# One pipeline over eight chunks for output projection, layer norm, shared expert and routing; expert weights split during the experts' stage; routing transfers moved

## The chip, the cores and the metric

The kernel runs on one core of one Trainium2 chip. The metric is device time in microseconds (us), the median of three runs. A profile is one execution recorded by the hardware profiler; its span runs from the first to the last instruction.

The engines are TensorE (PE; its weight loads are PEld), VectorE (DVE), ScalarE (ACT), GpSimd (POOL) and SyncE (SP), which here only issues transfers (its queue is SPq). TensorE has a granted clock of two levels, 1.2 and 2.4 GHz, written 0.50 and 1.00.

## What is computed

Two transformer layers on 4 x 1024 tokens of width 256, all in float32:

```python
x = x + attn0(layernorm(x))      # 16 heads of 16, causal softmax, then  o @ W_O.T
x = x + ffn0(layernorm(x))       # 32 experts, grouped top-8, latent width 128, plus a shared expert
x = x + attn1(layernorm(x))      # linear attention with decay, 16 heads of 128, RMS norm, gate
x = x + ffn1(layernorm(x))       # 48 kept experts of 128, top-8, capacity 96

# ffn0, what matters here
scores = sigmoid(x @ gate_w.T);  sb = scores + gate_bias
group_scores = top_k(sb grouped 4 x 8, 2).sum();  2 of 4 groups stay;  top 8 of the rest
w = scores at the top 8, divided by their sum, times 2.5
x_lat = x @ fc1_w.T
h = relu(x_lat @ w1[e].T)**2 * w[e]          # for each of 32 experts
routed = (sum over e of h @ w2[e].T) @ fc2_w.T
shared = relu(x @ shared_up_w.T)**2 @ shared_down_w.T
```

## The kernel before

Each stage is a `Phase`: it owns its tiles and semaphores, and at its end all engines meet at a barrier. Inside a phase each engine has its own instruction list, ordered by hand, and semaphores tie the lists together. The 4096 tokens are 32 tiles of 128 rows (`X[128, 32, 256]`, resident), or 8 chunks of 512. A float32 matrix product is made of three products of halves: the operand copied to `F32R` (the "high" part, on ACT) and the rest (the "low" part, a subtraction on DVE or POOL).

In the middle of the kernel stand these phases, one after the other:

- `trA` (`transpose_phase`, L230 to L262): the attention's output `AO` is transposed, all 8 chunks, into high and low halves.
- `proj` (`output_phase`, L789 to L811): the product with W_O for 32 tiles, each added to `X`.
- `lnB` (`transpose_phase`): mean and variance (L182, L185), square root on ACT (L245), normalised rows (L254), transposes (L230), halves (L262, L203).
- `shared` (`shared_phase`): per chunk the latent product and four inner products (L906), relu and square on ACT (L882, L887), then the second product (L923, full float32, recorded as two matmuls each), added to `X` (L962). After the last chunk come the gate's logits, 192 matmuls that stream 32 columns each (L940), and one sigmoid (L895).
- `route` (`group_routing_phase`): on DVE a chain of some forty operations over all 32 tiles at once (L1047 to L1090), each waiting for the one before; beside it the 4 MB of expert weights come in eight loads (L1020) and are split by ACT (L1104) and POOL (L1032). The square roots of the weights are transposed (L1096) and stored to `B_roots` (L1024).
- `experts` (`experts_phase`): for each of 8 chunks and 32 experts, three `up` matmuls (L1250 to L1252), weighing by roots and squaring (L1176, L1222, L1223, low part L1183 on DVE or, each fourth, L1210 on POOL), three `down` matmuls (L1259 to L1265). The roots come as 64 broadcast loads of 1 MB (`experts_sq`, L1150), four buffers ahead. The fc2 weight is loaded behind the first four of them (L1155), and PE waits for it before the loop. Twice a chunk `out` multiplies by fc2 (L1273).
- `lnC` and `lin`: the second attention, untouched in its loops. At its end DVE adds the 32 tiles of the result to `X` (L1666).
- `rank` (`ranking_phase`): an eight-chunk pipeline already. SP's list begins with the gate weight, the store of all of `X` to `out` (L1790) and the zero fills of `out`, `token_rows` and `odd_sums` (L1792 to L1797), and only then the stores of the normalised rows (L1803), which free the two `lines` buffers of ACT (L1980). DVE builds the one-hot tile `A` with twelve compares (L2081).
- `kept`: gather, products and scatter of the 48 experts, untouched.

## Time and profile before

| | us |
|---|---|
| median of three runs (3235.17 to 3238.91) | 3237.99 |
| the profiled execution | 3233.19 |
| its span | 3231.4 |
| attention of layer 0, start to 652 | 652 |
| trA, proj, lnB, shared, route: 652 to 952 | 300 |
| experts: 952 to 1358 | 406 |
| lnC, lin: 1358 to 2890 | 1532 |
| rank: 2890 to 3042 | 152 |
| kept: 3042 to the end | 189 |

Stage limits are read from the first and last instructions of each phase. Views list groups by line and engine, instructions in order of time, or busy time by stretch; "[x <-y]" at the end of a row is the idle time before it and what ended it. Busy times of pipelined matmuls overlap, so PE's pace is read from the distance of their starts.

### The profile page before, as it was taken

How to read it: one execution, taken by the hardware profiler on the slowest of the kernel's cores; microseconds unless marked ns; L12 is line 12 of the kernel's file. 1: busy time of each engine (PE TensorE's matmuls, PEld its weight loads, DVE VectorE, ACT ScalarE, POOL GpSimd, SP SyncE). 2: the span in 40 equal slices, each digit the busy share in tenths (PEclk: the TensorE clock that was granted, in tenths of full speed). 3: DMA queues.
4: the chain of work that ended last, by engine and by line, in shares of the span. 5: the costliest groups of instructions: out<-in, count | busy, mean ns of one | idle time of the engine just before them, and what ended most of it. 6: DMA issues, size and time to landing. Idle time of an engine off the chain costs nothing. (4 is left out here: it accounts for less than half of the span.)

```text
span 3231.4 us, 51793 instructions
## 1 busy us (share of the span) xinstructions
PE 2842.1 (88%) x17676; PEld 2278.6 (71%) x17676; DVE 1793.6 (56%) x3257; ACT 1451.9 (45%) x2661; POOL 773.7 (24%) x797
## 2 busy tenths in 40 slices
PE   5599999968918999879999999999999999967484
PEld 4544444457916878668888888888888888856463
DVE  5288888552166878755555555555555545554421
ACT  5247777744126877643333333333333333324110
POOL 2411222200021222112222222222222222213575
PEclk9889999978758999979999999999999999975665
DMA  4875555000037999500000000000000000023376
GB/s 149 231 100 71 73 74 81 3 19 0 1 90 157 178 184 174 119 11 10 10 10 2 8 10 10 10 10 10 10 10 9 1 10 10 8 68 98 74 173 125
DMA packets 183382, 193.61 MB, mean 60 GB/s; under 512 B 18080, under 2 KB 135360, under 8 KB 182720
## 3 DMA queue, kind: packets, MB, share of 16 engines
q1 hardware_dynamic: 174736, 177.10, 26.2%
q0 software_dynamic: 8544, 15.22, 2.8%
q8 instruction: 55, 0.90, 0.1%
q14 instruction: 47, 0.39, 0.1%
HBM read 149.89 MB, written 46.58 MB: 61 GB/s over the span
## 5 line engine op out<-in xcount | busy, mean ns | idle before, releaser
L744 DVE TENSOR_REDUCE score_pm<-score_SM 128x1 f32<-128x512 f32 (+3 forms) x608 | 364.5, 656 | 123.9 <-PE score_SM L613 73.7
L1423 POOL TENSOR_TENSOR lin_o2sum<-lin_o2sum,lin_o 128x512 f32<-128x512 f32 x128 | 165.7, 1295 | 1046.9 <-ACT lin_o L1459 1046.9
L704 ACT ACTIVATE score_PR<-score_SE 128x512 f32<-128x512 f32 (+1 forms) x640 | 309.9, 557 | 105.6 <-PE score_SE L638 102.1
L1638 DVE SCALAR_TENSOR_TENSOR lin_go<-lin_gT,lin_O 128x512 f32<-128x512 f32 x128 | 88.1, 688 | 477.8 <-ACT lin_o L1459 477.8
L1494 PE MATMUL lin_PJ<-C_XH,lin_WH 128*128 128x512 f32 x1032 | 341.6, 412 | 13.1 <-DVE lin_WL L1598 13.1
L1494 PE MATMUL lin_PJ<-C_XH,lin_WL 128*128 128x512 f32 x1032 | 320.5, 392 | 0.0
L1494 PE MATMUL lin_PJ<-C_XL,lin_WH 128*128 128x512 f32 x1032 | 320.4, 392 | 0.0
L610 PE MATMUL score_SM<-score_KR,score_QR 96*128 96x512 bf16 (+3 forms) x768 | 230.1, 341 | 28.3 <-DMA score_V<-v_rows 25.5
L1655 DVE TENSOR_TENSOR lin_acc<-lin_OUT,lin_acc 128x512 f32<-128x512 f32 x256 | 177.1, 692 | 139.9 <-PE lin_OUT L1529 138.7
L1442 ACT ACTIVATE lin_qT<-lin_PJ 128x512 f32<-128x512 f32 x129 | 77.1, 598 | 378.5 <-PE lin_PJ L1494 378.5
L1494 PEld LDWEIGHTS lin_PJ<-C_XL,lin_WH 128*128 128x128 f32 x1032 | 194.0, 188 | 43.2
L1494 PEld LDWEIGHTS lin_PJ<-C_XH,lin_WL 128*128 128x128 f32 x1032 | 194.0, 188 | 42.7
L1650 DVE TENSOR_TENSOR lin_gol<-lin_go,lin_goh 128x512 fp32r<-128x512 f32 x128 | 200.6, 1567 | 24.4 <-ACT lin_goh L1464 14.7
L638 PE MATMUL score_SE<-score_QR,score_KR 99*128 99x512 bf16 (+3 forms) x768 | 210.5, 330 | 2.0 <-ACT score_PR L704 1.5
L1222 ACT ACTIVATE experts_h<-experts_z 128x512 f32<-128x512 f32 x256 | 161.1, 629 | 109.5 <-DVE experts_z L1176 89.3
L1494 PEld LDWEIGHTS lin_PJ<-C_XH,lin_WH 128*128 128x128 f32 x1032 | 175.6, 190 | 34.7 <-DVE lin_WL L1598 13.5
L1176 DVE SCALAR_TENSOR_TENSOR experts_z<-experts_HP,experts_sq 128x512 f32<-128x512 f32 x256 | 172.2, 686 | 49.7 <-PE experts_HP L1252 26.7
L1560 PE MATMUL lin_O<-lin_sd,lin_v 128*128 128x128 f32 x1024 | 190.9, 276 | 6.3 <-issue 6.3
L1418 POOL TENSOR_TENSOR lin_qd<-lin_qT,lin_dec 128x512 f32<-128x512 f32 x128 | 166.0, 1297 | 84.3 <-DVE lin_dec L1620 73.9
L1562 PE MATMUL lin_O<-lin_qd,lin_kv 128*128 128x128 f32 x896 | 173.2, 275 | 0.0
L1560 PEld LDWEIGHTS lin_O<-lin_sd,lin_v 128*128 128x128 f32 x1024 | 159.7, 191 | 18.9 <-issue 9.7
L1210 POOL TENSOR_TENSOR experts_hl<-experts_h,experts_hh 128x512 fp32r<-128x512 f32 x64 | 83.0, 1296 | 344.5 <-ACT experts_hh L1223 336.8
(342 smaller groups left out, 6444.8 us busy)
## 6 DMA issues: line engine op xcount, KB each, us to landing
experts_sq<-B_roots SPq DMA_DIRECT2D x64, 1024.0 KB, 16.8
score_QR<-q_parts SPq DMA_DIRECT2D x96, 128.0 KB, 7.0
score_KR<-k_parts SPq DMA_DIRECT2D x96, 128.0 KB, 7.7
kept_GU<-L_ffn_gate_up_proj SPq DMA_DIRECT2D x48, 192.0 KB, 2.9
v_rows<-qkv_vt SPq DMA_DIRECT2D x32, 256.0 KB, 2.6
score_V<-v_rows SPq DMA_DIRECT2D x16, 512.0 KB, 10.8
C_w<-L_attn_w_qkv SPq DMA_DIRECT2D x51, 128.0 KB, 2.2
q_parts<-qkv_parts SPq DMA_DIRECT2D x16, 384.0 KB, 2.7
```

What stands on the lines that cost most here:

```text
L610: ins = nc.tensor.matmul(SM[:, count % RING, at:at + nk], QR[0:ROWS_QK, u, h0 + j, t * P:(t + 1) * P], KR[0:ROWS_QK, u, h0 + j, k0:k0 + nk ...
L638: ins = nc.tensor.matmul(SE[:, e % RING, at:at + nq], KR[0:ROWS_ALL, u, h, kt * P:(kt + 1) * P], QR[0:ROWS_ALL, u, h, q:q + nq], start=Tru ...
L704: nc.scalar.activation(PR[:, st % BUFS, h, 0:width], SE[:, e % RING, 0:width], ACT.Exp, scale=SCALE)\
L744: nc.vector.tensor_reduce(pm[:, n % 2, h0:h0 + nh, t, k0 // CHUNK], SM[:, count % RING, 0:nh * nk].rearrange("p (h k) -> p h k", h=nh), AX ...
L1176: nc.vector.scalar_tensor_tensor(z[:, e % 2], HP[:, e % BUFS], 0.0, sq[:, (e // QE) % BUFS, e % QE], ALU.max, ALU.mult).then_inc(dve_z, 1)
L1418: nc.gpsimd.tensor_tensor(qd[:], qT[:, u], dec[:, 0:1, :].to_broadcast([P, B4, BLK]), ALU.mult).then_inc(pool_qd, 1)
L1423: nc.gpsimd.tensor_tensor(o2sum[:, c], o2sum[:, c], o2[:], ALU.add).then_inc(pool_sum, 1)
L1494: ins = nc.tensor.matmul(PJ[:, bank], a[:, w, k, :], x[:, k, :, c, :], start=(n == 0), stop=(n == 3 * KD - 1))
L1560: ins = nc.tensor.matmul(O[:, b, :], v[:, b, :], sd[:, b, :], start=True, stop=(c == 0))
L1562: ins = nc.tensor.matmul(O[:, b, :], kv[:, b, :], qd[:, b, :], start=False, stop=True)
L1650: nc.vector.tensor_tensor(gol[:], go[:], goh[:].bitcast(F32), ALU.subtract).then_inc(dve_gol, 1)
L1655: nc.vector.tensor_tensor(dst, OUT[:, half], dst, ALU.add).then_inc(dve_acc[half], 1)
```

## The change

1. `output_phase`, the `lnB` transposes, `shared_phase` and `group_routing_phase` become one `front_phase`. In step i of ten, PE handles chunk i (transpose of AO, projection), chunk i-1 (transpose of the normalised rows, gate logits) and chunk i-2 (latent, inner and second products). The logits are made transposed, as 32 rows by 512 columns, so six 512-column matmuls a chunk replace 24 of 32 columns; the sigmoids are transposed back. Routing runs on DVE in four batches of 8 tiles, its pieces laid between the other work of the steps.
2. The expert weights: the first eight experts are loaded during `front`; the other loads, and all splits, are in `experts`. POOL does most of them in the first chunk. fc2 is loaded in `front` too.
3. The zero fills go to `front`; the ranking gate's loads go to `lnC`; the store of `X` to `out` is done by chunk, each behind the store of that chunk's rows.
4. The last addition of `lin` moves into the ranking stage, two chunks at a time ahead of their statistics. The twelve compares of `A` become one `tensor_tensor`.

```diff
+def front_phase(nc, a, AO, X, LH, LL, first_w, roots, ident, out, odd, rows):
+        @block.sync: loads wo, wu (2), wg, down, bias, then first_w (w1, w2 of experts 0 to 7, fc2), the four zero fills,
+            for c in range(CHUNKS):
+                sp.wait_ge(act_ro, c + 1)
+                sp.dma_start(roots[:, c * CHUNK:(c + 1) * CHUNK], rootT[:, c % 2])...
+        @block.tensor
+            for i in range(STEPS):                       # CHUNKS + 2
+                at_a, at_n, at_f = now(i, 0), now(i, 1), now(i, 2)
+                rooting = i - 5 if i >= 5 and i % 2 else None
+                attended(at_a)                           # 8 transposes of AO
+                latent(at_f); inner(at_f, 0); inner(at_f, 1)
+                normalised(at_n)                         # 8 transposes, waits lines_ready
+                inner(at_f, 2); inner(at_f, 3)
+                root_columns(rooting)                    # waits roots_ready
+                projection(at_a)
+                gates(at_n)
+                root_columns(rooting + 1)
+                second(at_f)
+                score_rows(at_n, i)
+            root_columns(CHUNKS - 2, CHUNKS)
+            root_columns(CHUNKS - 1, CHUNKS)
+        @block.vector
+            for i in range(CHUNKS + 1):
+                starts = (i - 3) // 2 if i >= 3 and i % 2 else None
+                ends = (i - 4) // 2 if i >= 4 and i % 2 == 0 else None
+                attended_low(at_a); latent_low(at_f)
+                group_sums(starts); refined_roots(starts - 1)
+                top_experts()                            # ends
+                low(at_n)
+                add_projection(at_a); variances(at_a)
+                add_second(at_f, 0); group_ranks(); add_second(at_f, 1)
+                scales(at_a); group_masks()
+                add_second(at_f, 2); add_second(at_f, 3); shares(ends)
+            last, b = CHUNKS - 1, CHUNKS // 2 - 1
+            latent_low(last); group_sums(b); refined_roots(b - 1); add_second(last, 0); group_ranks()
+            group_masks(); add_second(last, 1); top_experts(); add_second(last, 2); shares(b)
+            add_second(last, 3); refined_roots(b)
...
 def experts_phase
-            for q in range(BUFS):
+            load(0, 0)
+            load_weights(1, 0)
+            load_weights(1, 1)
+            for q in range(1, BUFS):
                 load(0, q)
-            sp.dma_start(fc2[:], a["L0_ffn_fc2_w"]).then_inc(w_in, 16)
+            (load_weights(2, w) behind dve_wl, load_weights(3, w) behind pool_wl)
...
+            for w, e in LOWS[0:4]:                       # POOL, chunk 0: 12 lows, 8 highs, between its eight `low`
+                weight_low(w, e)
+            low(0, 3)
+            weight_high(0, 16)
...
+            for q in range(2):                           # ACT, before its loop
+                for w in range(2):
+                    if q == 1:
+                        act.wait_ge(raw_in[q * 2 + w], 16)
+                    nc.scalar.activation(HIGH[w][:, q * WG:(q + 1) * WG, :], wraw[:, q, w], ACT.Copy)...
...
 def linear_attention_phase
-            for t in range(TILES):
-                nc.vector.scalar_tensor_tensor(X[:, t, :], acc[:, t, :], rs[:, t:t + 1], X[:, t, :],
-                                               ALU.mult, ALU.add)
 def ranking_phase, SP
-            sp.dma_start(o2n[0], o2n[1]).then_inc(o_loaded, 16)
-            sp.dma_start(raw[0], raw[1]).then_inc(g_loaded, 16)
-            sp.dma_start(out[0:T, :].rearrange("(t p) n -> p t n", p=P), X[:]).then_inc(stored, 16)
-            (the four zero fills)
             for i in range(STEPS): ... store of lines, chunk g
+                    sp.wait_ge(x_ready, (g + 1) * TPC)
+                    sp.dma_start(out[g * CHUNK:(g + 1) * CHUNK, :]..., X[:, tiles_of(g), :])
 def ranking_phase, DVE
             def variances(run):
                 for t in tiles:
+                    nc.vector.scalar_tensor_tensor(X[:, t, :], acc[:, t, :], rs[:, t:t + 1], X[:, t, :],
+                                                   ALU.mult, ALU.add).then_inc(x_ready, 1)
+                for t in tiles:
                     nc.vector.bn_stats(stats[:, t, :], X[:, t, :]).then_inc(stats_ready, 1)
             variances(0)
+            scales(0)                                    # was behind the seven casts and `perm`
-                    for v in range(HI):
-                        ins = ts(A[:, g % 3, :, v, :], ..., float(v), None, ALU.is_equal)
+                    tt(A[:, g % 3], places.to_broadcast([P, TPC * EG, HI, 8]),
+                       step_no[:].to_broadcast([P, TPC * EG, HI, 8]), ALU.is_equal).then_inc(dve_a, 1)
```

## Rows read from the trace of the kernel before

**Rows 1.** The page: busy time of each engine over the whole span.
```profile
PE 2842.1 (88%) x17676; PEld 2278.6 (71%) x17676; DVE 1793.6 (56%) x3257; ACT 1451.9 (45%) x2661; POOL 773.7 (24%) x797
```

**Rows 2.** Busy time by stretch; lnB, shared, route, experts.
```profile
core 0: us, PE busy (x) PEld busy (x) DVE busy (x) ACT busy (x) POOL busy (x), PEclk, DMA share, GB/s
702.00:738.00 36.00, 15.71 (x64) 12.54 (x64) 23.31 (x81) 25.29 (x45) 0.00 (x0) 0.51 0.11 32
738.00:890.00 152.00, 148.19 (x688) 131.69 (x688) 20.76 (x42) 46.74 (x76) 0.00 (x0) 0.87 0.00 0
890.00:952.00 62.00, 6.48 (x32) 4.45 (x32) 46.28 (x130) 14.85 (x14) 20.49 (x8) 0.53 0.27 77
...
981.00:1357.00 376.00, 372.06 (x1607) 301.06 (x1608) 293.01 (x458) 287.52 (x512) 81.69 (x63) 0.99 0.86 167
```

**Rows 3.** PE in order of time: transposes, projection, inner products, second product.
```profile
663.61 1.09 PE L230 MATMUL trA_tr<-ident,trA_rows 128*128 128x128 f32 x8 [0.76 <-DVE A_XL L203]
681.30 0.46 PE L800 MATMUL proj_Y<-proj_WH,A_XH 128*128 128x256 f32 x2
...
682.80 0.46 PE L800 MATMUL proj_Y<-proj_WH,A_XH 128*128 128x256 f32 x2
...
835.13 0.62 PE L906 MATMUL shared_HP<-B_XH,shared_WH 128*128 128x512 f32 x2
835.59 0.62 PE L906 MATMUL shared_HP<-B_XL,shared_WH 128*128 128x512 f32 x2
...
837.86 13.97 PE L923 MATMUL shared_OP<-B_w_down,shared_su 128*128 128x256 f32 x64
```

**Rows 4.** Busy time by stretch, inside the shared stage: before and in the logits.
```profile
837.00:851.00 14.00, 14.00 (x66) 12.29 (x65) 2.98 (x7) 3.43 (x5) 0.00 (x0) 1.00 0.00 1
...
856.00:889.00 33.00, 32.64 (x154) 32.53 (x153) 0.00 (x0) 0.33 (x1) 0.00 (x0) 0.50 0.00 0
```

**Rows 5.** Groups by line, 700 to 1150 us: costs that the steps repeat.
```profile
L203 DVE TENSOR_TENSOR B_XL<-lnB_tr,B_XH 128x1024 fp32r<-128x1024 f32 x8 | 9.8, 1223 | 10.1 <-ACT B_XH L262 10.1
...
L962 DVE TENSOR_TENSOR X<-shared_OP,X 128x256 f32 (+1 forms) x32 | 13.6, 425 | 72.6 <-PE shared_OP L923 72.6
...
L1087 DVE RECIPROCAL route_inv<-route_root 128x1024 f32<-128x1024 f32 x1 | 6.6, 6552 | 1.1 <-ACT route_root L1106 1.1
...
L895 ACT ACT_TABLE_LOAD x1 | 1.3, 1283 | 0.0
```

**Rows 6.** DVE and POOL in order of time in the routing stage.
```profile
896.51 2.60 DVE L1052 TENSOR_TENSOR route_hi<-route_hi 128x256 f32<-128x256 f32 x1
...
901.63 0.42 DVE L1054 TENSOR_TENSOR route_u<-route_lo 128x256 f32<-128x256 f32 x1
...
896.49 4.83 POOL L1032 TENSOR_TENSOR B_W1L<-route_raw,B_W1H 128x1024 fp32r<-128x1024 f32 x2 [257.79 <-ACT B_W1H L1104]
```

**Rows 7.** Experts: PE's first wait, and two stretches, one of them in routing.
```profile
982.49 0.79 PE L1250 MATMUL experts_HP<-B_LH,B_W1H 128*128 x1 [23.83 <-DMA experts_fc<-L_ffn_fc_w]
...
1165.00:1210.00 45.00, 44.58 (x190) 34.77 (x189) 34.18 (x55) 34.11 (x62) 9.78 (x8) 1.00 1.01 184
...
900.00:922.00 22.00, 0.00 (x0) 0.00 (x0) 21.31 (x93) 5.49 (x6) 14.51 (x6) 0.50 0.49 143
```

**Rows 8.** End of lin and head of rank, in order of time: DVE, SP, ACT, PE.
```profile
2876.66 12.75 DVE L1666 SCALAR_TENSOR_TENSOR X<-lin_acc,lin_rs,X 128x256 f32<-128x256 f32 x32
...
2902.34 15.94 SPq L1797 DMA_DIRECT2D odd_sums<-rank_zero  x1
...
2927.73 2.08 ACT L1980 ACTIVATE rank_lines<-X,rank_shift,rank_rstd 128x256 f32<-128x256 f32 x4 [21.28 <-DMA token_rows<-rank_lines]
...
2903.35 1.94 PE L1905 MATMUL rank_tr<-ident,rank_lines 128*128 128x128 f32 x8 [4.90 <-ACT rank_lines L1980]
...
2932.11 1.94 PE L1905 MATMUL rank_tr<-ident,rank_lines 128*128 128x128 f32 x8 [16.24 <-DVE rank_XL L2073]
...
2959.90 2.80 DVE L2081 TENSOR_SCALAR rank_A<-rank_hi 128x192 bf16<-128x192 bf16 x12
```

877 lines of the change are left out of this document (556 added, 321 removed).

## Prediction, made before the changed kernel was built or timed

> **What bounds the kernel now.** The page first: PE is busy 88% of the span [rows 1], so the time to be won is where PE is idle, at half clock, or on work that costs more than it must. The view by stretch shows where [rows 2]. From 652 to 952 us lie five stages in a row, and each has another limit: in trA and lnB PE, ACT and DVE hand a chunk round (in lnB PE is busy 16 of 36 us, at a clock of 0.51); in the shared stage PE is the bound (148 of 152 us); in routing PE does 6.5 of 62 us while DVE works off its chain. Within the shared stage the clock tells of waste: it is 1.00 while products of 256 and 512 columns run, and 0.50 through the logits, though PE is busy 32.6 of 33 us there [rows 4]; those 192 matmuls of 32 columns last from 851.5 to 889, about 37 us. The experts' stage is bound by PE (clock 0.99, busy 372 of 376 us), with the transfers just behind: a DMA share of 1.01 at 184 GB/s in the middle [rows 7]. Ahead of it stands a wait of 23.8 us for the small fc2 weight, which is queued behind 4 MB of roots [rows 7]. In rank, ACT waits 21.3 us for a `lines` buffer, because SP is stuck for 15.9 us issuing a zero fill [rows 8].
>
> **Part 1, the front pipeline.** What PE must do for one chunk at full clock, from starts [rows 3]: eight transposes 1.1 us, twice (2.2); the projection, two tiles in 682.80 - 681.30 = 1.50, so four tiles 3.0; latent, four inner and the gates, six groups of six 512-column matmuls 0.227 apart (835.59 - 835.13 = 0.46 for two), 6 x 1.36 = 8.2; the second product, 64 records from 837.86 in 13.97 us, so 32 in 6.8 (its last 0.2 overlap); scores and roots, eight small transposes, at most 1.1. Sum 21.3 us; I take 21.2 for a full step.
>
> Do the others fit under it? DVE per step: the two low halves 2 x 1.22 and the latent one 0.69, projection and second additions 8 x 0.425 = 3.4 [rows 5], variances and scales about 2.4 (estimated: half of lnB's 3.5 us for eight tiles, and some waits): 8.9. The routing: DVE is busy 46.3 us in the routing stage [rows 2]. Of this about 10 us is not work: L1052 takes 2.60 us where L1054, the same shape, takes 0.42, and it starts with a POOL subtraction of 2.4 us (two take 4.83) [rows 6]; five operations in the view are longer by 2.0 to 2.2 us in this way. 36 / 4 = 9 us for a batch of 8 tiles, plus about forty times 0.1 us, since small operations don't shrink with their size: 13 to 14 us per two steps. They aren't even: odd steps hold the sums, ranks, masks and refined roots (a reciprocal of 6.55 / 4 = 1.6 us [rows 5] among them), some 9.5, even steps 4.8. DVE is then at 18.4 of 21 in odd steps, 13.7 in even ones. ACT: halves 2.0, latent 0.6, four relu and square 4.9, sigmoid 0.6, rows 2.1, roots and copies 1.3, sqrt 0.2 and, as the work alternates between sigmoid and sqrt, two table loads of 1.28 [rows 5]: 14.3. So PE stays the bound.
>
> Where the lists touch: in odd steps from 5 on PE waits with `root_columns` for DVE's refined roots. Behind them on DVE stand the shares of the last step (to 2.7 us into the step), the two low halves (4.6), the sums (8.0) and the roots (11.1), while PE is there at 8.7: 2.4 us lost, in steps 5 and 7. Queued behind PE's wait are projection, gates and second product, all of them. The normalised rows are ready at the step's end and wanted 5 us into the next, so that handover is hidden; without that cover the 2.4 would grow by what it is late.
>
> The stretch, step by step. Steps 0 and 1 have no products of a third chunk to hide anything: loads and splits of W_O (about 5.5 us), projection at half clock 5.1, statistics and rows 5.6, transposes, halves, projection, gates, scores 11: 27.5 us, step 2 starts at 680. Steps 2 to 7: 6 x 21.2 + 2 x 2.4 - 1.6 (no roots yet in the first three) = 130, to 810. Step 8 has no new chunk: 16.6, to 827. Step 9 and the tail go by DVE: second product begun at 11, ranks, masks, top 8 and shares of the last batch between the additions to 22, refined roots 25.5, two transposes and copies 28, store and barrier 31.3: 858. The first root load of the experts' stage, now at 952.8, comes at 858: **95 us less**. Bounds: 108 less if steps cost 19.5 us (starts overlap better) and the tail 27; 60 less if each of seven steps costs 5 us more.
>
> **Part 2, the experts.** Removed: the wait for fc2 (23.8 us), during which the root buffers stay full or arrive unused. Added: 6 weight loads of 0.5 MB in the first chunk, and splits on ACT, DVE and POOL ahead of it or in it. Price of a load: the routing stage moved 143 GB/s at a share of 0.49 [rows 7], so 290 GB/s when busy, 1.8 us each, 11 us in all. Roots: 1.05 MB at 184 GB/s = 5.7 us each; the first four took 6.7 (982.49 less 952.8 and 2 us for the first to come, by 4.1 MB). The first chunk needs eight of them and the weights: 2 + 8 x 6.1 + 11 = 62 us, where PE's work is 44: it is bound by transfers. The other 56 root loads follow at 5.7 us (PE's own pace for four experts is 4 x 6 x 0.227 + 0.2 = 5.65, so it can't be faster by much): 319. Then the last four experts and the tail, 14: 395 us against 405 now. **10 less**; bounds +5 (roots at 160 GB/s in the first chunk and every later stall kept) to 20 less (PE as the only bound after 16 us). ACT's loop starts behind the second pair of weight loads, about 14 us in; this is under the roots' arrival. POOL's 12 lows, 8 highs and 8 own lows at 1.3 us are 36 of 62 us. DVE's low halves will at times wait as L1052 did, 24 x up to 1.3 us: DVE 19 + 24 x 1.9 = 65 us at the very worst, 3 us over the transfers. I take 0.
>
> The Trainium skill ("SBUF — State Buffer", Who interferes with whom) speaks against this edit: a DVE operation with two inputs in SBUF and a GpSimd operation that reads SBUF shut each other out for a whole instruction. By that rule, the trace agrees (2.60 against 0.42 us), and in the first chunk the sum would be 3 us longer.
>
> **Part 3, rank.** Now: roots of the RMS norm ready at 2876.6, 12.75 us of additions [rows 8], barrier, first transposes at 2903.35, third group at 2932.11 after a 16.2 us wait. After: barrier to 2878, memset 0.9, eight additions 3.2, statistics 3.5, scales: first rows at 2886. PE's list first needs the permuted gate, behind casts and `variances(1)` with another 3.2: transposes at 2896, second 2900, third 2909. From there as now, 109 us, plus some 3 us for the additions of later runs: end at 3021 instead of 3041. **20 less.** The cover: the out stores, now one 0.5 MB store per chunk, 2 to 4 us in steps of 11. If they block as now, it is 4 less instead of 20. `A` costs 2.80 us in twelve compares [rows 8]; one operation of 2304 elements costs from 1.3 to 2.5 us, plus up to 3.1 when POOL's product is in flight (twelve short ones meet it too, up to 4.7 us in the last chunks); I take 0, bounds -1.5 to +1 per chunk, DVE having 4 us spare per step. Zero fills in the front: 4.3 MB beside no other transfer, hidden. Gate loads in lnC, hidden.
>
> **Sum.** 95 + 10 + 20 = 125 us. The profiled execution has span 3231.4 and time 3233.2; so span 3106, time 3108. The median stands 4.8 above that execution: **3113 us**.
>
> **Rivals.** *Handovers rule the pipeline* (each of seven steps 4 to 7 us longer, since nine waits of three hand-ordered lists are met in one order only): for it, the odd steps, where DVE has 2.6 us spare by my count; against it, the 5 us slack of the rows. 3113 + 28 to 49: about 3150. *The ranking stall moves instead of going*: 3113 + 16 = 3129. *The experts' transfers don't fit* (stall kept, or POOL late with the third weight group): 3113 + 15 = 3128. *Everything overlaps better* (13 in the front, 10 in the experts): 3090. *Slower than before*: the pipeline runs at half clock. Step 2 to the end of PE's work is 130 + 17 + 14 = 161 us at full clock; each of them at half costs as much again: 3113 + 161 = 3274. It takes a clock of 0.50 in 78% of it (125 of 161 us) to lose the whole gain. For it: lnB at 0.51 and the logits at 0.50 with PE busy [rows 2, 4]; against: the dense stretch at 1.00 [rows 4], which is made of the same matmuls, and the transposes and small groups are 1 to 2 us long between them. The Trainium skill ("TensorE: Matmul & The Clock Gate", HAM oscillation) says that a PE that pauses between bursts falls back to half clock again and again; the trace agrees in lnB, and it would make 3274 if each step paused long enough.
>
> **Chances.** Forecast 0.64 (own range 3095 to 3128), handovers 0.16, rank stall 0.06, experts 0.07, better 0.05, half clock 0.02. Range for 8 in 10: 3085 to 3150. A measurement can tell about 0.2% (6 us) from no change. Faster 0.97, the same 0.01, slower 0.02; the front alone would have to lose 95 us for the middle case.
>
> **What would show it.** Front: first root load at 858, steps 21.2 us apart by their gates, clock 1.00 from step 2 on, PE waiting only for refined roots in steps 5, 7 and 9. Experts: PE never waits for fc2 but for roots in the first chunk, which lasts 62 us; 395 us in all. Rank: no wait of ACT for `token_rows`, 145 us from the roots of the norm (2876.6 now) to the last index. It is wrong if steps exceed 25 us, if the clock is 0.50 inside them, or if later chunks of the experts lack roots by more than 15 us in all.

## The result and the profile after

The changed kernel takes 3124.61 us (median of 4 runs, 3122.50 to 3126.47), the kernel before 3238.15 us on the same chip (4 runs, 3235.17 to 3238.91): a ratio of 0.9651, 95% interval 0.9634 to 0.9668, or 113.5 us less. The forecast was 3113 us, range 3085 to 3150. The profiled execution took 3125.01 us with a span of 3123.2 us, against 3233.19 and 3231.4 before.

A stage is measured here from one event to the next: start, first root load of the experts, first load of the next layer norm, roots of the RMS norm ready, first load of the kept experts, end.

| stretch | before, us | after, us | difference | forecast |
|---|---|---|---|---|
| up to the first root load (the front) | 952.8 | 856.9 | -95.9 | -95 |
| experts | 406.8 | 416.6 | +9.8 | -10 |
| layer norm and linear attention | 1516.8 | 1518.0 | +1.2 | 0 |
| ranking (the additions are within it in both) | 166.2 | 142.6 | -23.6 | -20 |
| kept experts | 188.9 | 189.2 | +0.3 | 0 |
| sum | 3231.5 | 3123.3 | -108.2 | -125 |

Two of the three terms came within 4 us, the third has the wrong sign. These are single profiles: in the seven profiles whose front is the same code, the first root load comes at 856.6 to 859.7 us. These are the rows of the change. First the whole span, which answers to [rows 1]:

```profile
PE 2817.1 (90%) x17564; PEld 2237.4 (72%) x17564; DVE 1800.2 (58%) x3284; ACT 1463.9 (47%) x2689; POOL 792.0 (25%) x812
```

TensorE was busy 25 us less, and the span is 108 us shorter: three quarters of the gain is time in which TensorE had been idle. By stretch, the front (it answers to [rows 2]; start, length, busy time of PE, PEld, DVE, ACT, POOL, granted clock, DMA share, GB/s): its head, steps 2 to 7, step 8, step 9 with the tail.

```profile
652.00:680.00 28.00, 16.19 (x86) 14.36 (x87) 11.43 (x32) 11.21 (x15) 3.60 (x3) 0.67 0.85 251
680.00:808.00 128.00, 124.38 (x686) 103.73 (x684) 80.58 (x273) 83.50 (x132) 0.00 (x0) 1.00 0.02 4
808.00:825.00 17.00, 17.00 (x83) 13.26 (x81) 6.04 (x32) 8.58 (x13) 0.00 (x0) 1.00 0.00 0
825.00:857.00 32.00, 18.07 (x81) 12.92 (x79) 19.96 (x74) 9.92 (x17) 0.00 (x0) 0.86 0.04 9
```

The pace of the steps stands in TensorE's order of time, at the transposes that open each step, and, in odd ones, at those of the refined roots:

```profile
700.90 1.09 PE L936 MATMUL front_TR<-ident,AO 128*128 128x128 f32 x8
721.35 1.09 PE L936 MATMUL front_TR<-ident,AO 128*128 128x128 f32 x8
741.81 1.09 PE L936 MATMUL front_TR<-ident,AO 128*128 128x128 f32 x8
752.20 0.61 PE L1031 MATMUL front_RT<-ident,front_root 128*32 128x128 f32 x4 [1.42 <-DVE front_root L1277]
764.74 1.09 PE L936 MATMUL front_TR<-ident,AO 128*128 128x128 f32 x8
...
850.59 1.03 PE L1031 MATMUL front_RT<-ident,front_root 128*32 128x128 f32 x4 [6.59 <-DVE front_root L1277]
```

These are the openings of steps 3 to 6. Steps 3, 4 and 6 take 20.45 us, step 2 takes 21.4, steps 5 and 7 take 22.9. The last root transposes at 850.6 wait 6.6 us for VectorE; that is the tail.

In the experts' stage, the first chunk in order of time on POOL, PE and SP's queue, and then 45 us of the later chunks by stretch:

```profile
878.37 1.30 POOL L1451 TENSOR_TENSOR experts_hl<-experts_h,experts_hh 128x512 fp32r<-128x512 f32 x1 [2.48 <-ACT experts_hh L1513]
892.36 1.52 POOL L1461 TENSOR_SCALAR B_W1H<-B_wraw 128x512 fp32r<-128x512 f32 x1 [12.68 <-DMA B_wraw<-L_ffn_w]
...
896.65 1.26 POOL L1451 TENSOR_TENSOR experts_hl<-experts_h,experts_hh 128x512 fp32r<-128x512 f32 x1
...
897.97 0.79 PE L1564 MATMUL experts_Y<-experts_hl,B_W2H 128*128 128x512 f32 x1 [10.69 <-POOL experts_hl L1451]
...
858.62 11.59 SPq L1376 DMA_DIRECT2D experts_sq<-B_roots  x3
870.25 22.13 SPq L1380 DMA_DIRECT2D B_wraw<-L_ffn_w  x4
```

```profile
1065.00:1110.00 45.00, 44.44 (x191) 35.24 (x191) 36.70 (x58) 35.70 (x65) 9.21 (x8) 1.00 1.01 169
```

The 23.8 us of [rows 7] are gone. In their place TensorE waits 10.7 us for a low half of GpSimd (expert 7's), which stands in GpSimd's list behind the first copy of the third weight group; that copy waits 12.7 us for its transfer, and SyncE needs 22 us to issue four transfers. In the later chunks the DMA share is 1.01 at 169 GB/s; VectorE waited 25.0 us for roots from 927 to 1260 us, in 21 waits.

In ranking (it answers to [rows 8]): DVE, SP and PE in order of time, then the group of the comparison for `A`.

```profile
2793.79 3.20 DVE L2306 SCALAR_TENSOR_TENSOR X<-C_acc,C_rs,X 128x256 f32<-128x256 f32 x8
...
2803.30 0.37 SPq L2086 DMA_DIRECT2D token_rows<-rank_lines  x1
2803.73 0.50 SPq L2089 DMA_DIRECT2D out<-X  x1
...
2810.35 1.94 PE L2189 MATMUL rank_tr<-ident,rank_lines 128*128 128x128 f32 x8 [5.62 <-DVE rank_GL L2346]
...
2831.36 1.91 PE L2189 MATMUL rank_tr<-ident,rank_lines 128*128 128x128 f32 x8
2843.76 1.94 PE L2189 MATMUL rank_tr<-ident,rank_lines 128*128 128x128 f32 x8 [3.72 <-DVE rank_XL L2361]
```

```profile
L2369 DVE TENSOR_TENSOR rank_A<-rank_hi,rank_step_no 128x2304 bf16<-128x2304 bf16 x8 | 14.7, 1835 | 6.8 <-POOL rank_lo L2165 6.8
```

The same group in the kernel before, twelve a chunk:

```profile
L2081 DVE TENSOR_SCALAR rank_A<-rank_hi 128x192 bf16<-128x192 bf16 x96 | 30.4, 389 | 6.8 <-POOL rank_lo L1879 6.8
```

SyncE isn't held up any more, the first transposes come 19.0 us after the roots of the norm (2791.4) instead of 27.0, and the single comparison for `A` takes 1.84 us on average, where twelve took 3.8 (30.4 us in eight chunks; the 2.80 us of [rows 8] are one chunk of them, and they range from 1.5 to 5.6).

### The profile page after: what moved, and what is told of

Read it like the earlier page. It is cut to its first block and busy times, and to the rows that moved or that the text cites. A ratio compares the mean times of both kernels' runs of the same rounds, so it can differ in the third digit from the quotient of the medians.

```text
span 3123.2 us, 51426 instructions
## 1 busy us (share of the span) xinstructions
PE 2817.1 (90%) x17564; PEld 2237.4 (72%) x17564; DVE 1800.2 (58%) x3284; ACT 1463.9 (47%) x2689; POOL 792.0 (25%) x812
## 5 line engine op out<-in xcount | busy, mean ns | idle before, releaser
L1950 DVE TENSOR_TENSOR C_acc<-lin_OUT,C_acc 128x512 f32<-128x512 f32 x256 | 177.1, 692 | 141.9 <-PE lin_OUT L1824 139.6
L1737 ACT ACTIVATE lin_qT<-lin_PJ 128x512 f32<-128x512 f32 x129 | 76.9, 596 | 376.1 <-PE lin_PJ L1789 376.1
L1424 DVE TENSOR_TENSOR experts_hl<-experts_h,experts_hh 128x512 fp32r<-128x512 f32 x192 | 138.3, 720 | 49.7 <-ACT experts_hh L1513 40.7
## 6 DMA issues: line engine op xcount, KB each, us to landing
experts_sq<-B_roots SPq DMA_DIRECT2D x64, 1024.0 KB, 17.7
```

The lines of the kernel that those rows point to most:

```text
L1950: nc.vector.tensor_tensor(dst, OUT[:, half], dst, ALU.add).then_inc(dve_acc[half], 1)
```

## The experiments

The runs of one group share a chip with runs of the kernel before, whose median lay between 3233 and 3237 us in them; kernels of different groups are therefore compared by their ratio to it. Within the experts' stage, time is told by the copies of each chunk's sum (`experts_y`) on ScalarE: "first chunk" is from the first root load to the copy of chunk 0, "seven chunks" from there to the copy of chunk 7.

| kernel | median, us | ratio to before, 95% | first chunk | seven chunks | experts' stage |
|---|---|---|---|---|---|
| before | 3238.15 | 1 | 76.9 | 324.0 | 406.8 |
| changed | 3124.61 | 0.9651 (0.9634 to 0.9668) | 80.2 | 330.8 | 416.6 |
| pool_order | 3124.47 | 0.9649 (0.9633 to 0.9665) | 77.0 | 328.1 | 410.6 |
| sp_order | 3123.35 | 0.9647 (0.9631 to 0.9663) | 74.5 | 330.7 | 410.7 |
| two_groups | 3114.11 | 0.9617 (0.9601 to 0.9633) | 68.2 | 331.7 | 405.1 |
| half_roots | 3112.11 | 0.9612 (0.9596 to 0.9628) | 79.9 | 315.7 | 401.2 |
| distinct_rows | 3094.90 | 0.9574 (0.9558 to 0.9590) | 63.8 | 315.7 | 385.1 |
| chunk_major | 3095.33 | 0.9567 (0.9551 to 0.9583) | 62.7 | 315.7 | 383.9 |
| four_copies | 3107.39 | 0.9609 (0.9593 to 0.9625) | 73.8 | 315.7 | 395.0 |
| adds_back | 3123.42 | 0.9663 (0.9647 to 0.9679) | 79.8 | 325.0 | 410.3 |
| rank_back | 3143.60 | 0.9720 (0.9704 to 0.9736) | 80.2 | 328.5 | 414.3 |
| columns_late | 3123.37 | 0.9657 (0.9641 to 0.9674) | 79.5 | 327.2 | 412.2 |
| before_fc2_first | 3223.55 | 0.9972 (0.9962 to 0.9982) | 63.7 | 329.8 | 399.3 |
| before_chunk_major | 3210.97 | 0.9925 (0.9908 to 0.9941) | 61.0 | 317.5 | 384.2 |

The last three columns are from one profile each; in before_fc2_first they start at the load of fc2, 0.5 us ahead of the first root load. Three kernels leave something out of the result: two_groups half of the expert weights, half_roots half of the roots, distinct_rows all of the roots. Four kernels have the changed kernel's experts' stage word for word (changed, adds_back, rank_back, columns_late): it took 416.6, 410.3, 414.3 and 412.2 us. So the +9.8 us of the first table is +6.5 us on average (413.3 less 406.8), with a scatter of 3 us either way, nearly all of it in the seven later chunks; the first chunk repeats to 0.7 us. The kernel before has one profile only, and that execution lay 5 us under its median, so the loss itself is uncertain by some us: with the medians (113.5 us less) and all other stages as in the first table it would be 4.5 us.

### Why does the first chunk take 80 us?

pool_order puts two of GpSimd's own low halves first, and moves three later ones (15, 19 and 23) up with them.

```diff
             low(0, 3)
+            low(0, 7)
+            low(0, 11)
             weight_high(0, 16)
             weight_low(0, 16)
             weight_high(0, 20)
-            low(0, 7)
...
```

> The changed kernel with two of GpSimd's own low halves, of experts 7 and 11, put ahead of the first weight group it has to wait for. In the changed kernel the experts' stage lasts 416.6 us (first root load to the next layer's first load), of which the first chunk takes 80.2 us up to the copy of its sum. Theory A (the order alone: TensorE stands still for 10.7 us only because expert 7's low half is queued behind a weight copy that waits for its transfer): first chunk 70 us, whole kernel about 10 us faster than the changed one. Theory B (GpSimd has 33 us of work left from the landing of the third weight group at 892.4 us, so only an earlier landing helps): TensorE's wait moves to the later weight groups, first chunk 77 us, 3 us faster at most. Theory C (the first chunk is bound by transfers as a whole): 80 us, no change.

First chunk 77.0 us, theory B. The wait did not go, it moved. TensorE's rows, and one of VectorE's:

```profile
898.09 0.49 PE L1547 MATMUL experts_HP<-B_LH,B_W1H 128*128 x1 [1.57 <-POOL B_W1L L1470]
...
916.60 0.79 PE L1547 MATMUL experts_HP<-B_LH,B_W1H 128*128 x1 [3.62 <-POOL B_W1L L1470]
...
905.33 1.29 DVE L1417 SCALAR_TENSOR_TENSOR experts_z<-experts_HP,experts_sq 128x512 f32<-128x512 f32 x2 [5.62 <-DMA experts_sq<-B_roots]
```

TensorE now waits for low halves of later weights, and VectorE 5.6 us for the fifth root load, which SyncE could issue only behind the weight groups. Over the whole kernel nothing of it is left that can be measured (0.9649 against 0.9651).

sp_order leaves GpSimd's list alone and interleaves the loads.

```diff
             load(0, 0)
             load_weights(1, 0)
             load_weights(1, 1)
-            for q in range(1, BUFS):
-                load(0, q)
+            load(0, 1)
+            load_weights(2, 0)
+            load(0, 2)
+            load_weights(2, 1)
+            load(0, 3)
+            (load_weights(2, w) still behind dve_wl, load_weights(3, w) behind pool_wl)
...
+            (first round of the root loop written out, load_weights(3, w) behind its loads 0 and 1)
```

> The changed kernel with GpSimd's list as it was, but SyncE issues the third weight group between the first root loads instead of behind all four, and the fourth group between root loads five to seven. Theory A (order of GpSimd's list alone): the copy still waits for its landing, which is some 12 us earlier, so it gains too, about 10 us; it cannot be told from B here, but is by pool_order. Theory B (landing of the third group, then 33 us of GpSimd work): the third group lands at about 878 to 880 instead of 892, first chunk 68 us instead of 80.2, whole kernel 12 us faster. Theory C (first chunk bound by the bytes it moves, whatever their order): 80 us, no change.

First chunk 74.5 us, half of what theory B promised, and not theory C's 80:

```profile
883.72 1.95 POOL L1466 TENSOR_SCALAR B_W1H<-B_wraw 128x512 fp32r<-128x512 f32 x1 [1.17 <-DMA B_wraw<-L_ffn_w]
...
906.36 1.49 POOL L1466 TENSOR_SCALAR B_W1H<-B_wraw 128x512 fp32r<-128x512 f32 x1 [6.95 <-DMA B_wraw<-L_ffn_w]
...
909.13 0.79 PE L1569 MATMUL experts_Y<-experts_hl,B_W2H 128*128 128x512 f32 x1 [6.11 <-POOL experts_hl L1456]
```

The third group came early enough (a wait of 1.2 us), and now the fourth was late: GpSimd waits 7.0 us for it and TensorE 6.1 us for the low half behind it. In both orders some load is late. So the order of the queue is worth 6 us of this chunk and the order of GpSimd's list 3; the rest looks like a stretch limited by its transfers, which the later runs bear out. Both edits together were not run.

two_groups leaves half of the experts' weights out.

```diff
-            (load_weights(2, w), load_weights(3, w))
-            (weight_high(w, e), weight_low(w, e) for e of 16 to 31)
-                nc.tensor.matmul(HP[:, s], W1H[:, e, :], LH[:, cols], start=True, stop=False)
+                nc.tensor.matmul(HP[:, s], W1H[:, e % 16, :], LH[:, cols], start=True, stop=False)
...
```

> The changed kernel without the third and fourth weight groups: their four loads and GpSimd's twelve splits (eight high copies and eight low halves less the four of the second group) are left out, experts 16 to 31 are computed with the weights of 0 to 15, and the rest is as it was, so its output is not the reference's. It prices the split of the weights inside the experts' stage. Theories A and B: the first chunk falls from 80.2 to 60 to 64 us (16 us to the first product, then TensorE's own pace), 16 to 20 us faster. Theory C (bytes): 2 MB fewer at about 290 GB/s, 7 us faster. The later chunks stay at 330.8 us in all if their pace has nothing to do with the first chunk.

(GpSimd's instructions left out are sixteen, eight high copies and eight low halves, not twelve.) First chunk 68.2 us, 12.0 less: between the theories (16 to 20 by A and B, 7 by C). So loading and splitting half of the weights costs 12 us here; the two were not told apart. The seven later chunks stay at 331.7 us, as expected.

### What sets the pace of the later chunks?

half_roots takes half of the bytes away from the fifth root load on. (It was meant to begin with the second chunk; but `first` holds only for the four loads ahead of SyncE's loop, so the second half of the first chunk has half loads too.)

```diff
-                src = roots[q * QE:(q + 1) * QE, bass.ds(g * CHUNK, CHUNK)]
+                first = isinstance(g, int) and g == 0
+                n = QE if first else QE // 2
+                src = roots[q * QE:q * QE + n, bass.ds(g * CHUNK, CHUNK)]
...
```

> The changed kernel with only half of the bytes of each root load from the second chunk on: two of the four experts' roots are loaded, the other two are left from the first chunk, so its output is not the reference's. Copy of chunk 0 to copy of chunk 7 takes 330.8 us in the changed kernel (7 chunks of 47.3 on average, DMA share about 1.00 at 170 to 177 GB/s). If transfers set the later chunks' pace: they fall to TensorE's own 45 us, 313 to 316 us in all, 15 to 18 us faster. If the hand-over between TensorE, VectorE and ScalarE sets it: 328 to 331 us, no change. The first chunk stays at 80 us.

Seven chunks take 315.7 us instead of 330.8, and each of the five inner ones 45.34 or 45.35 us, where in the changed kernel they varied from 46.4 to 49.1. The transfers set the pace; TensorE's own is 45.35 us. The first chunk stays at 79.9 us though four of its eight root loads are halved: what delays it lies ahead of the fifth load.

distinct_rows brings as many bytes in as many pieces, from other addresses.

```diff
-                src = roots[q * QE:(q + 1) * QE, bass.ds(g * CHUNK, CHUNK)]
-                sp.dma_start(sq[:, q % BUFS], src.rearrange("(o e) n -> o e n", o=1).to_broadcast([P, QE, CHUNK]))\
+                src = distinct[q % BATCH].rearrange("(e p w) d -> p e w d", e=QE, w=2)
+                sp.dma_start(sq[:, q % BUFS].rearrange("p e (w d) -> p e w d", w=2), src)\
```

> The changed kernel in which each root load brings the same number of bytes in the same pieces (128 partitions, four pieces of 2 KB each), but every partition reads its own 2 KB of the kernel's input instead of all 128 reading the same 2 KB of roots; the mixture is weighed with wrong numbers, so its output is not the reference's. The later chunks take 330.8 us for seven in the changed kernel, 315.7 where half of the bytes were left out. Theory R (the repeated source is what holds the transfers at 170 to 184 GB/s): the loads get faster, seven chunks 316 to 319 us, whole kernel 12 to 15 us faster than the changed one. Theory B (the bytes into the partitions hold it, wherever they come from): 328 to 333 us, no change.

Theory R, and more of it than expected: 315.7 us for the seven chunks and 63.8 for the first, which none of the theories had put down to the source. So the bytes into the partitions, and the number of pieces, are not the limit; where they are read from is. Whether that is because all partitions read the same rows or because of how the rows lie in memory isn't shown by this run, which changes both and the tensor besides. An edit that keeps the result right, and all partitions reading the same rows, is chunk_major:

```diff
-        roots = nc.dram_tensor("B_roots", (EXPERTS, T), F32, kind="Internal").ap()
+        roots = nc.dram_tensor("B_roots", (CHUNKS * EXPERTS, CHUNK), F32, kind="Internal").ap()
...
-                sp.dma_start(roots[:, c * CHUNK:(c + 1) * CHUNK], rootT[:, c % 2]).then_inc(stored[c % 2], 16)
+                sp.dma_start(roots[c * E:(c + 1) * E, :], rootT[:, c % 2]).then_inc(stored[c % 2], 16)
...
-                src = roots[q * QE:(q + 1) * QE, bass.ds(g * CHUNK, CHUNK)]
+                src = roots[bass.ds(g * E + q * QE, QE), :]
```

> The changed kernel with the roots laid out in memory chunk by chunk, so that the four experts' roots of one load lie side by side: a partition reads one piece of 8 KB instead of four of 2 KB, still the same for all 128. Distinct sources took seven later chunks from 330.8 to 315.8 us. Theory P (16 DMA engines reading the same 2 KB at the same time hold each other up; over 8 KB they spread out): seven chunks 316 to 325 us, whole kernel 8 to 25 us faster than the changed one. Theory Q (what counts is that one place in memory serves all partitions, however long the piece): 326 to 333 us, no change.

Theory P, with all that could be had: ratio 0.9567 against 0.9651 for the changed kernel, 27 us of 3238 (a little more than the 25 that the theory allowed). One row each of the changed kernel, of distinct_rows and of chunk_major from the view of the DMA issues (count, size, median us from issue to landing); then 45 us by stretch, of distinct_rows and of chunk_major, and in chunk_major PE's wait for GpSimd in the first chunk (us in total, times, longest):

```profile
experts_sq<-B_roots SPq DMA_DIRECT2D x64, 1024.0 KB, 17.7
```

```profile
experts_sq<-L_attn_x SPq DMA_DIRECT2D x64, 1024.0 KB, 5.2
```

```profile
experts_sq<-B_roots SPq DMA_DIRECT2D x64, 1024.0 KB, 4.7
```

```profile
1065.00:1110.00 45.00, 45.00 (x200) 37.28 (x199) 37.10 (x58) 36.75 (x65) 10.35 (x8) 1.00 0.54 183
```

```profile
1065.00:1110.00 45.00, 45.00 (x201) 37.27 (x199) 37.44 (x58) 36.82 (x65) 10.01 (x9) 1.00 0.50 180
```

```profile
PE experts_Y L1564 <- POOL experts_hl L1451: 1.9, 3, 0.7
```

The same megabyte lands in 4.7 us instead of 17.7, and the DMA share of that stretch is 0.50 instead of 1.01 for a like rate. The 17.7 us contain the wait behind earlier loads that were still under way; the first root load of the stage, with none ahead of it, landed after 10.4 us in the changed kernel and 4.7 in chunk_major. PE waits 1.9 us in all for GpSimd in the first chunk instead of 11.4, and the chunk takes 62.7 us instead of 80.2, with GpSimd's list and SyncE's order unchanged. So the slow root loads, behind which the weights had to wait, made the first chunk long; the two orders only decided how much of that reached TensorE.

four_copies spreads the readers instead.

```diff
...
+                for k in range(COPIES):
+                    part = slice(k * P // COPIES, (k + 1) * P // COPIES)
+                    src = roots[k, q * QE:(q + 1) * QE, bass.ds(g * CHUNK, CHUNK)]
+                    src = src.rearrange("(o e) n -> o e n", o=1).to_broadcast([P // COPIES, QE, CHUNK])
+                    sp.dma_start(sq[part, q % BUFS], src).then_inc(sq_in[q % BUFS], 16)
```

> The changed kernel with four copies of the roots in memory, and each root load split in four transfers of 32 partitions, each from a copy of its own. 1.5 MB more is stored in the front, in eight steps. If repetition of an address over the whole load is what costs (128 readers of one row, now 32): seven chunks 316 to 325 us, whole kernel 8 to 25 us faster. If what costs is that the 16 engines read the same rows at the same moment (they take the four transfers one after the other, so they still do): 326 to 333 us, no change or, with the stores in the tail of the front, 1 to 2 us slower.

```profile
1065.00:1110.00 45.00, 45.00 (x200) 37.28 (x199) 37.12 (x58) 36.56 (x65) 10.34 (x8) 1.00 0.77 187
```

The seven chunks are at TensorE's pace here too, by a DMA share of 0.77, so four copies with a quarter of the readers each help as well; the first chunk (73.8 us) gains less than half as much as with the new layout. Why the old source is slow isn't settled by this. Readers per row, readers at one moment, the length of a piece (2 or 8 KB) and the 16 KB from one expert's row to the next were not told apart: chunk_major changes the last two together, four_copies the first together with the size of a transfer (256 KB).

### Was the wait for fc2 lost time?

before_fc2_first is the kernel before with one load moved.

```diff
+            sp.dma_start(fc2[:], a["L0_ffn_fc2_w"]).then_inc(w_in, 16)
             for q in range(BUFS):
                 load(0, q)
-            sp.dma_start(fc2[:], a["L0_ffn_fc2_w"]).then_inc(w_in, 16)
```

> The kernel before with one edit: the small fc2 weight is loaded ahead of the four root loads instead of behind them, so TensorE's 23.8 us wait goes. The stage lasted 406.8 us. Theory S1 (transfers set the pace of the whole stage, the wait for fc2 lay beside 4 MB of roots that had to come anyway): 402 to 407 us, whole kernel 0 to 5 us faster. Theory S2 (the wait is TensorE's own lost time, as the prediction has it): TensorE starts 13 us earlier and the stage ends 13 us earlier, at 394 us. It tells besides why seven later chunks took 324.0 us before and 330.8 after: 324 again if it is the place of the data in memory, 329 or more if it is that the transfers have no head start any more.

399.3 us, 7.5 less by one profile each; the medians of ten and thirteen executions on one chip differ by 9.7 us (3233.21 and 3223.55; 5.8 to 12.3 by the interval of the ratio), which is more than S1 allows. So it is between S1 and S2: the wait was worth 7.5 to 10 us. TensorE's first chunk ends 13.2 us earlier (63.7 against 76.9 us), and the seven others then take 329.8 instead of 324.0, so part of the thirteen is given back; how much isn't fixed by one profile, since the seven chunks of the changed kernel's code scatter from 325.0 to 330.8. VectorE's waits from 950 to 1030 us show where:

```profile
DVE experts_z L1176 <- DMA experts_sq<-B_roots: 15.1, 6, 8.7
```

Against 8.0 us in one wait from 952 to 983, and none from 983 to 1040, in the kernel before. While TensorE stood, the four buffers had filled; without that head start it runs into the transfers.

before_chunk_major gives the kernel before the new layout of the roots (the load as in chunk_major, the store in pieces of two chunks).

> The kernel before with the roots laid out in memory chunk by chunk, as in chunk_major, and nothing else changed; fc2 is still loaded behind four root loads, and all weights are still split in the routing stage. Its experts' stage lasted 406.8 us, that of the changed kernel 416.6 and with the new layout 383.9. It tells what the change's edits to the experts' stage are worth once the root loads are out of the way. Theory K (the old layout hid what the change wins there; freed of it the wait for fc2 shrinks to a few us by itself, since four loads take some 5 us each to land): the stage takes 380 to 386 us, as long as in the changed kernel or a little less, so those edits win nothing in this stage in either layout, and the whole kernel is 21 to 27 us faster than before. Theory L (the fc2 wait stays TensorE's own loss of 13 us or more, and with the loads out of the way the change wins the 10 us that the prediction gave it): the stage takes 392 to 396 us.

384.2 us, theory K, and the whole kernel 24 us faster. The wait for fc2 has shrunk by itself:

```profile
965.90 0.79 PE L1251 MATMUL experts_HP<-B_LH,B_W1H 128*128 x1 [8.09 <-DMA experts_fc<-L_ffn_fc_w]
```

With the new layout the experts' stage takes 384.2 us before the change and 383.9 after. So what the change does there wins no time in this stage in either layout. What it does bring is that three quarters of the loads and all splits of the weights no longer stand in the front, and with the new layout that costs nothing.

### Ranking and the odd steps

adds_back returns the additions to the end of the linear attention:

```diff
+            for t in range(TILES):
+                nc.vector.scalar_tensor_tensor(X[:, t, :], acc[:, t, :], rs[:, t:t + 1], X[:, t, :],
+                                               ALU.mult, ALU.add)
...
             def variances(run):
-                (the additions of this run, and the wait for them)
```

> The changed kernel with the 32 additions of the linear attention's result put back to the end of its stage, out of the ranking; everything else of the ranking as changed. From the roots of the norm to the end of the ranking the changed kernel takes 142.6 us, the kernel before 165.9 (23.3 less). Theory D (the additions and the transfers each have their share): 12.75 us of additions come back ahead of all, two times 3.2 go from the first tiles' path, so 150 to 155 us, 9 to 13 us slower than the changed kernel. Theory T (the transfers account for all of it, the additions only moved): 143 to 146 us.

145.3 us (2785.6 to 2930.9), 2.7 more than changed: theory T. Three of its rows show why it is so little:

```profile
2785.98 12.76 DVE L1961 SCALAR_TENSOR_TENSOR X<-C_acc,C_rs,X 128x256 f32<-128x256 f32 x32
...
2811.01 1.94 PE L2192 MATMUL rank_tr<-ident,rank_lines 128*128 128x128 f32 x8 [2.45 <-DVE rank_GL L2345]
...
2840.74 1.94 PE L2192 MATMUL rank_tr<-ident,rank_lines 128*128 128x128 f32 x8 [0.17 <-DVE rank_XL L2360]
```

The first transposes come 25.4 us after the roots of the norm, against 19.0: 6.4 us are lost at the head. But from the fourth transposes to the fifth it takes 8.9 us (2831.88 to 2840.74), where the changed kernel takes 12.4 (2831.36 to 2843.76), since a run of eight additions lies between them there: 3.5 us come back.

rank_back returns the transfers as well:

```diff
+            sp.dma_start(out[0:T, :].rearrange("(t p) n -> p t n", p=P), X[:]).then_inc(stored, 16)
+            (the four zero fills, taken out of the front)
...
-                    sp.dma_start(out[g * CHUNK:(g + 1) * CHUNK, :].rearrange("(t p) n -> p t n", p=P),
-                                 X[:, tiles_of(g), :]).then_inc(stored, 16)
```

> The changed kernel with the additions put back as in adds_back and also the zero fills and the one 4 MB store of the result put back to the head of the ranking's transfers. Both theories: the wait of ScalarE for its rows is back, about 166 us from the roots of the norm to the end of the ranking, 20 to 24 us slower than the changed kernel. Theory D: the difference to adds_back is 11 to 16 us, theory T: 20 us or more. If the single comparison for the one-hot table matters too, it ends a few us below 166, since that edit stays: 158 to 164.

```profile
2816.61 16.31 SPq L2085 DMA_DIRECT2D odd_sums<-rank_zero  x1
```

```profile
ACT rank_lines L2265 <- DMA token_rows<-rank_lines: 21.6, 1, 21.6
```

161.7 us, 16.4 more than adds_back and 19.1 more than changed, a little under the 20 to 24 of both theories; the 16.4 is just past theory D (11 to 16) and well short of theory T (20 or more). So adds_back came out as T had it and this one as D had it: the additions cost little, the transfers 16 us, and the rest is neither. SyncE's block of 16.3 us and ScalarE's wait of 21.6 us are those of [rows 8]. It ends 4.5 us short of the kernel before (166.2). Of this 1.6 us lie ahead of the first transposes (25.4 after the roots instead of 27.0). The gate's load, also moved, isn't what they waited for, since the permuted gate comes later here than in the kernel before (21.5 us after the roots, 20.7 before); the rows of ScalarE come earlier, 19.4 us after the roots instead of 23.0, since `scales(0)` and the rows now stand ahead of the casts and of the gate's copy. This order was not run by itself. Another 3.1 us lie behind the third transposes (107.2 to the end instead of 110.4), where the comparison for `A` is the only edit left.

columns_late moves the transposes of the refined roots.

```diff
-                if rooting is not None:
-                    root_columns(rooting, min(i - 1, CHUNKS))
                 if at_a is not None:
                     projection(at_a)
                 if at_n is not None:
                     gates(at_n)
+                (root_columns(rooting, min(i - 1, CHUNKS)) in steps 5 and 7)
...
                 (the second group inside second(), ahead of its second tile)
```

> The changed kernel with the transposes of the refined roots put later in TensorE's list in the odd steps: the first group behind the gates instead of ahead of the projection, the second behind the first tile of the second product. In the changed kernel an odd step of 5 and 7 takes 22.9 us and an even one 20.45; of the 2.5 us between them 1.4 us is TensorE's wait for VectorE's roots and about 1.1 us the transposes themselves. Theory W (only the wait is lost time, and nothing else is late behind it): steps 5 and 7 take 21.5 us each, the front 2.8 us less. Theory V (VectorE's list is what sets the odd steps): the wait comes back at another line, projection or second product, and the steps stay at 22.9 us.

```profile
741.09 1.09 PE L936 MATMUL front_TR<-ident,AO 128*128 128x128 f32 x8
752.95 0.51 PE L964 MATMUL front_YO<-front_WOH,front_AH 128*128 128x256 f32 x2 [1.50 <-DVE X L1200]
...
764.11 1.09 PE L936 MATMUL front_TR<-ident,AO 128*128 128x128 f32 x8
```

Step 5 takes 23.0 us (22.9 before the edit): theory V. The wait of 1.4 us for the roots has become one of 1.5 us for an addition of the projection, which stands behind those roots in VectorE's list.

## Why the prediction was right, and where it was not

**The front, right in its steps.** Head: step 2 forecast at 680, measured 679.5. Steps 2 to 7: forecast 130 us, measured 128.6 (679.5 to 808.1). Step 8: 17.0 against 16.6. Tail: 31.8 against 31.3. First root load: 856.9 against 858. The clock was 1.00 from 680 to 825, which ends the rival of the half clock and that of the handovers (no step over 22.9 us). Two parts of the working were not what they seemed. The odd steps are 2.5 us longer than the others, where 2.4 was forecast, but that these two agree is luck: the forecast was a wait of 2.4 us, and measured are a wait of 1.4 and 1.1 us for the eight root transposes, which the prediction had spread over all steps (so that its full step was 21.2 us and not 20.45). And the wait isn't one for the roots alone: put behind the gates (columns_late), it comes back as 1.5 us for the projection's additions, so VectorE's list up to there sets it; the budget of "18.4 of 21" was the warning. The rule of the Trainium skill ("TensorE: Matmul & The Clock Gate", HAM oscillation), that a pausing PE falls back to half clock again and again, was met in the front only in the head (0.67) and the tail (0.86), where PE is busy 58 and 56% of the time.

**The experts, wrong: forecast -10, measured +9.8 in the profile and +6.5 on average.** The prediction's sum for the stage was 62 us until the eighth root load has landed, 319 for the other 56 loads, and 14 from the last landing to the end. By the landings in the traces these were 65.9, 336.2 and 14.4 us (65.3, 333.0 and 15.0 on average of the four profiles), and in the kernel before 60.3, 330.4 and 16.1. So the term that failed is the price of a root load: 5.7 us from the best stretch of [rows 7] (184 GB/s), where the 56 loads took 5.9 each in the kernel before already and 5.9 to 6.0 after. With the mean of before in place of the best stretch, 62 + 330 + 14 = 406, the working itself would have forecast no gain. Its own sign of being wrong, more than 15 us of missing roots in later chunks, was met: VectorE waited 25.0 us for them. The other comparison made there was right, "PE's own pace" of 5.65 us per load: it is 45.35 / 8 = 5.67, so that the fault lay in taking transfers and PE for equally fast.

The 62 us held for the roots but not for TensorE, whose last product of the first chunk starts at 77.9, 12 us behind that landing. What it lost there are the 10.7 us of waiting for GpSimd and some us of half clock, for which the sum has no term: the granted clock was 0.59 from 858 to 878 us and 0.56 from 898 to 903, behind that wait, against 0.87 in the first 19 us of TensorE's work in the kernel before (981 to 1000).

And what was to be won was less than it looked. "Removed: the wait for fc2 (23.8 us)" lay beside 4 MB of roots in a stage that its transfers limit, so that it was worth 7.5 to 10 us (before_fc2_first), and nothing at all where the roots load fast (384.2 against 383.9). What was put in its place cost 17.3 us (399.3 to 416.6 by single profiles, 14 on average), against 11 for the six loads in the prediction, because they stood in the queue behind slow root loads, and GpSimd's list, in which TensorE's low halves stand between copies that wait for a transfer, passed each delay on.

The words of the rival were "the experts' transfers don't fit (stall kept, or POOL late with the third weight group)", at 3128 us and a chance of 0.07: this is what happened, and 3124.6 lies nearer to it than to the forecast. It should have had several times that chance: a DMA share of 1.01 stood in the rows, and the edit adds six loads to the same queue.

VectorE's low halves did get longer in the first chunk, up to 1.72 us against 0.78 at most before, as the Trainium skill ("SBUF — State Buffer", Who interferes with whom) has it. In that chunk they took 23.6 us of VectorE's time instead of 18.6; what this cost the stage wasn't measured by itself, but chunk_major, where they took 25.3, has a first chunk of 62.7 us.

**Ranking, right in its main term.** Forecast -20, measured -23.6. Transfers: forecast 16, measured 16.4 (rank_back less adds_back). Head, up to the first transposes: forecast 7.4 earlier, measured 8.0, of which 6.4 by the additions and 1.6 by the order of the first rows. Additions of the later runs: forecast 3 back, measured 3.5, so that moving them gave 2.7 us in all. The comparison for `A` was put at 0 with bounds of -1.5 to +1 per chunk and gave 3.1 us in eight. The parts add up to 23.8, the stage to 23.6.

**The whole.** 95.9 + 23.6 - 9.8 - 1.5 in the other stages = 108.2 us between the profiles, 17 less than the 125 forecast. Between the medians it is 113.5, since the profiled execution of before lay 5 us under its median and that of after at its own; in which stage those 5 us lie isn't shown. That the time fell into the forecast's own range (3095 to 3128) although one of its three terms had the wrong sign is in part luck: front and ranking gave 4.5 us more than forecast, and these 5 us fell on the right side.

## What to carry to other kernels

A wait of the busiest engine is worth what the next resource leaves of it: before pricing it, ask whether a transfer that has to be made anyway lies beside it, and take the price of a transfer from the mean of the whole stage, not from its best stretch (here it was 5.9 us against 5.7, and 56 times this difference is all of the gain that was forecast). Where the DMA share is near 1 at half the rate that other transfers reach, look at the source before the order of the queue: the layout of one tensor in memory gave 27 us here, where reordering the queue and reordering GpSimd's list gave nothing that could be measured in the whole kernel. And in an engine's list, work for which the main engine waits should not stand behind an instruction that waits for a transfer, but moving it helps only if that transfer isn't what limits the stretch.

## What the runs showed of the hardware

A 1 MB load in which 128 partitions read the same four rows of 2 KB, 16 KB apart, took 17.7 us to land behind its predecessors (16.8 in the kernel before), and such loads ran at 169 to 184 GB/s with all DMA engines shown busy (a share of 1.01); with distinct rows, the same number and size of pieces, 5.2 us at a share of 0.54; with the four rows side by side in one piece of 8 KB, still the same for all partitions, 4.7 us at 0.50. Half as many rows from the old layout (512 KB) took 4.9 us. An estimate that leaves the waiting out, the rate of 1065 to 1110 us divided by the DMA share: 167 GB/s in the changed kernel, 211 in half_roots, 243 in four_copies, 339 in distinct_rows and 360 in chunk_major. The Trainium skill ("DMA: Bandwidth & Descriptors", Bandwidth) has transfers of 1 MiB and more at 75% of the peak and above (341 GB/s for 1 MB in its table, measured with transfers that GpSimd issues); the root loads of this kernel did not come near that until their source was changed. The same page (Latency and other measured facts) tells of a loss where the rows of the partitions are a large power of two apart, 512 KiB and more in its figures, and infers that they meet in the same memory channel; here the partitions were zero apart and the experts' rows 16 KB, which no run separates.

The loads limited by their source also made the time uneven: chunks of 44.2 to 50.2 us and 324 to 332 us for seven, where every kernel with fast loads had inner chunks of 45.34 or 45.35 us and 315.7 to 317.5 for seven.

SyncE, which issues a transfer in about 0.4 us, was held far longer while large transfers were queued: 11.6 us over three root loads, 22.1 us over four weight loads behind them, and 16.3 us over one zero fill behind the 4 MB store in rank_back. What stands behind on its list, the loads of the weights here and the stores of rows in the ranking, had to wait for it.
